# Fetching more of the gathered source rows by plain DMAs from SyncE and ScalarE in a two-layer graph kernel

## The reference

```python
h = relu(layernorm(x))
# layer 1
edge_in  = concat([h[src], h[dst], edge_attr])            # 128 + 128 + 64
edge_msg = relu(relu(edge_in @ We1 + be1) @ We2 + be2)    # 32, then 128
h2       = relu(concat([h[dst], edge_msg]) @ Wn1 + bn1)   # 64
node_msg = relu(h2 @ Wn2 + bn2)
x = x + h + segment_sum(node_msg, dst)
h = relu(layernorm(x))
# layer 2
msg = ((h @ W[etype])[src] + b[etype]) * edge_weight      # 8 relations
x = x + h + relu(segment_sum(msg, dst))
```

## Time and profile before

| what | before |
|---|---|
| median of 3 runs | 7919.92 us (7915.28 to 7920.59) |
| the profiled execution: time, span of its instructions | 7916.95 us, 7915.1 us |
| PE busy | 6812.1 us (86%) |
| POOL busy | 5850.2 us (74%) |
| DVE busy | 4295.3 us (54%) |
| ACT busy | 2361.7 us (30%) |
| indirect DMAs of layer 1 and of layer 2 | 3128 and 3055, 944 ns each |
| one-row DMAs issued by SP and by ACT (layer 2) | 6272 and 3072 |
| mean granted clock of PE | 0.94 |

### The profile page before, as it was taken

How to read it: one execution, slowest core, us unless ns; L and a number is a source line. 1 busy time by engine, 2 the same in 40 slices (tenths; PEclk the granted TensorE clock), 3 DMA queues, 4 the chain that set the end, 5 groups by cost and what they waited for, 6 DMA issues and landing times. The chain is left out here.

```text
span 7915.1 us, 215516 instructions
## 1 busy us (share of the span) xinstructions
PE 6812.1 (86%) x53038; PEld 5262.4 (66%) x53038; DVE 4295.3 (54%) x15013; ACT 2361.7 (30%) x7307; POOL 5850.2 (74%) x6213
## 2 busy tenths in 40 slices
PE   7999999999999999999978887787888887788777
PEld 6666666666666766666666666666666666666666
DVE  5445444454444544544455555555555555555555
ACT  5444444444444444444430000000000000000000
POOL 4777777777777777777757777777777777777776
PEclk8999999999999999999988889888888889988998
DMA  5333333333333333333322222222222222222222
GB/s 145 86 87 87 86 87 86 87 87 86 87 87 86 87 86 86 87 86 87 86 84 56 56 56 56 56 56 56 56 56 56 56 56 56 56 56 56 56 56 77
DMA packets 630304, 585.32 MB, mean 74 GB/s; under 512 B 306227, under 2 KB 505147, under 8 KB 629228
## 3 DMA queue, kind: packets, MB, share of 16 engines
q0 software_dynamic: 197856, 251.86, 15.3%
q1 hardware_dynamic: 422268, 325.27, 14.1%
q10 hardware_dynamic: 9600, 1.60, 0.1%
HBM read 558.88 MB, written 19.27 MB: 73 GB/s over the span
## 5 line engine op out<-in xcount | busy, mean ns | idle before, releaser
L617 POOL DMA_INDIRECT shared<-p_tab,idx x3128 | 2952.4, 944 | 1032.2 <-issue 1029.1
L617 POOL DMA_INDIRECT rows_place<-h_tab,idx x3055 | 2883.3, 944 | 945.3 <-issue 838.5
L1220 PE MATMUL bank<-shared,rows_place 128*128 128x256 f32 x6110 | 1803.2, 446 | 613.9 <-DMA rows_place<-h_tab,idx 602.6
L1220 PEld LDWEIGHTS bank<-shared,rows_place 128*128 128x128 f32 x6110 | 1273.0, 218 | 876.8 <-DMA rows_place<-h_tab,idx 659.4
L1037 DVE SCALAR_TENSOR_TENSOR shared<-bank,key,late 128x256 f32<-128x256 f32 x3128 | 1291.8, 476 | 808.4 <-PE bank L1222 667.4
L779 ACT ACTIVATE h_place<-bank 128x256 f32<-128x256 f32 x782 | 300.4, 384 | 3474.9 <-PE bank L1222 2840.5
L1131 PE MATMUL bank<-h_sb,w_tile 128*128 128x128 f32 x6256 | 908.6, 288 | 69.3 <-DVE h_sb L941 0.9
L1131 PEld LDWEIGHTS bank<-h_sb,w_tile 128*128 128x128 f32 x6256 | 759.3, 191 | 279.4 <-DVE h_sb L941 279.4
L941 DVE TENSOR_SCALAR h_sb<-bank,be_col 128x128 f32<-128x128 f32 x782 | 273.9, 350 | 1236.5 <-PE bank L1124 1236.5
L1150 PE MATMUL bank<-wn_half,h_sb 128*128 128x128 f32 x6256 | 890.8, 285 | 0.0
L1233 PE MATMUL bank<-h_place,w_rel_sb 128*128 128x64 f32 x6256 | 848.0, 293 | 0.0
(11 more groups left out here) (96 smaller groups left out, 6362.8 us busy)
## 6 DMA issues: line engine op xcount, KB each, us to landing
rows_place<-in_dst_c SPq DMA_DIRECT2D x782, 192.0 KB
h_place<-h_tab SPq DMA_DIRECT2D x6272, 0.5 KB
shared<-in_edge_cols SPq DMA_DIRECT2D x782, 128.0 KB
shared<-p_tab,idx POOLq DMA_INDIRECT x3128
h_place<-h_tab ACTq DMA_DIRECT2D x3072, 0.5 KB
rows_place<-h_tab,idx POOLq DMA_INDIRECT x3055
qr_f<-qr_tab SPq DMA_DIRECT2D x782, 36.0 KB
idx<-in_src_t SPq DMA_DIRECT2D x393, 8.0 KB
```

What stands on the lines that cost most here:

```text
L617: pool.indirect_dma_start(out=rows_of[s][:, t, :], out_offset=None, in_=table, in_offset=bass.IndirectOffsetOnAxis(ap=idx[k][:, s * TC + t ...
L1220: pe.matmul(bank[s][:, 0:RW], there, hot_rel[s % 2][:, t, :], start=(t == 0), stop=(t == TC - 1))
```

## The change

In layer 1, loops of `LONG` = 32 chunks take the place of those of 4 and 8 (`longs`, `pipelined`). In the last chunk of each of the 24 loop bodies (i = 33) POOL fetches only tiles 2 and 3. Tile 0 is fetched by SP and tile 1 by ACT, row by row, into the new tile `fed_p` (`RowFeed`). SP spreads its 128 rows over the steps 5 to 33 of the body, ACT over the steps 3 to 31, 4 or 5 rows per step. They read the numbers 8 at a time (`NUMBERS`), ACT ahead of `relu_msg1` and the rows behind it. PE sums the last chunk's source rows in four matmuls instead of one, and waits for both engines' rows. SP loads `dst_wide` and `qr_f` for the chunk two ahead (`LEAD`), and reads the windows' first nodes four at once. It loads `idx` one quad ahead instead of two, after the first gather of the running quad has landed.

In layer 2, SP's and ACT's tiles are both those of chunk 13 of each of the 49 superchunks (the last is the one that stops at chunk 13): tile 0 by SP as before, tile 1 by ACT, now 8 rows per chunk, two chunks earlier than SP. Chunk 15 is fetched by POOL in full. ACT's numbers come with SP's in one DMA of 256. POOL issues 3080 and 3030 indirect DMAs.

```diff
@@
-    ACT_ROWS = 5
-    ACT_FED_AT = SUP - 1
+    LONG = 32
+    NLONG = (NCH - 2) // LONG
+    FED_P = 2
+    LEAD = 2
+    NUMBERS = 8
...
+        def feed_step(eng, f, lead, u, lone, after, landed):
+
+            first = FED_AT - lead - SUP + 1
+            if u - first < SUP:
+                feed(eng, f, lone, u - first, landed)
+            elif after:
+                if u == first + SUP:
+                    eng.wait_ge(fed_ids_landed, 16 * after.ids_turn + 16)
+                    hold(eng)
+                feed(eng, f, after, u - first - SUP, landed)
...
+        def longs(eng, m, step):
+            for i in range(2):
+                step(Long(m, 0, i))
+            with eng.Fori(0, NLONG) as long:
+                for i in range(2, LONG + 2):
+                    step(Long(m, long, i))
+            for i in range(2 + LONG * NLONG, NCH):
+                step(Long(m, 0, i, tail=True))
...
+        class RowFeed:
+            def load_ids(self, at):
+                self.eng.dma_start(fed_p_ids[self.f][0:1, :], src_t[:, ds((at.long * LONG + LONG + 1) * TC + self.f, 1)].rearrange("p o -> o p"),
+                                   allow_slow_non_contiguous=True).then_inc(fed_p_ids_landed[self.f], 16)
+            def rows_at(self, at):
+                k = at.i - self.first if at and at.feeds else -1
+                return range(k * P // self.steps, (k + 1) * P // self.steps) if 0 <= k < self.steps else range(0)
+            def read_numbers(self, at):
+                for p in self.rows_at(at):
+                    if p % NUMBERS == 0:
+                        self.numbers[p:] = nc.values_load_multi_w_load_instructions(
+                            fed_p_ids[self.f][0:1, p:p + NUMBERS], engines=(self.eng.engine,), min_val=0, max_val=NPAD - 1,
+            def fetch(self, at):
+                for p in self.rows_at(at):
+                    self.eng.dma_start(fed_p[p:p + 1, self.f, :], p_tab[ds(self.numbers[p], 1), :]).then_inc(fed_p_landed[self.f], 16)
...
+                def load_window(at):
+                    c = chunk_of(m, at)
+                    s = c.slot
+                    sp.wait_ge(hot_built[s], c.turn + 1)
+                    hold(sp)
+                    sp.dma_start(dst_wide[s], dst_c[ds(c.i, 1), :].rearrange("c e -> (c e)").partition_broadcast(3 * W))\
+                      .then_inc(dst_wide_landed[s], 16)
+                    if s == 0:
+                        starts[:] = nc.values_load_multi_w_load_instructions(
+                            base_i[0:1, ds(c.i, SL)], engines=(sp.engine,), min_val=0, max_val=TOP,
+                    sp.wait_ge(split_hi[s], c.turn + 1)
+                    hold(sp)
+                    sp.dma_start(qr_f[s][:, :], qr_tab[ds(starts[s], W), :].rearrange("(a w) o -> a w o", a=1).broadcast_to([3, W, QR]))\
+                      .then_inc(qr_landed[s], 16)
+                feed_p = RowFeed(sp, 0, SL + 1, LONG + 1)
+                def step(at):
...
                     sp.dma_start(ea[s][:, :], edge_cols[ds(c.i, 1), :, :].rearrange("c p n -> (c p) n")).then_inc(ea_landed[s], 16)
+                    if s == 2 and at.i // SL + 1 < NQ:
+                        sp.wait_ge(prow_landed[0], 16 * TC * c.turn + 16 * TC)
+                        hold(sp)
+                        load_idx(c.quad + 1, 1 - at.i // SL % 2, idx_landed)
+                    if at.i + LEAD < NCH:
+                        load_window(Long(m, at.long, at.i + LEAD))
+                    if at.feeds and at.i == 2:
+                        feed_p.load_ids(at)
...
+                    feed_p.read_numbers(at)
+                    feed_p.fetch(at)
...
+            feed_p = RowFeed(act, 1, 3, LONG - 1)
...
+                feed_p.read_numbers(at)
                 if c:
                     relu_msg1(c)
+                feed_p.fetch(at)
                 if before:
                     relu_msg2(before)
...
+                feed_step(act, 1, 2, u, lone, after, act_row_landed)
...
+                if at.fed:
+                    for f in range(FED_P):
+                        pe.wait_ge(fed_p_landed[f], 16 * P * at.turn + 16 * P)
+                        pe.matmul(ps_h1[f * H1:(f + 1) * H1, 0:P], fed_p[:, f, :], ident[:, :], start=False, stop=True)
+                    for t in range(FED_P, TC):
+                        ins = pe.matmul(ps_h1[t * H1:(t + 1) * H1, 0:P], prow[s][:, t, :], ident[:, :], start=False, stop=True)
```

More of the change, by code:

```diff
@@ L373, in tiles_gathered @@
                 return TC * c.turn + TC
[L374 to L388, removed]
@@ L390, in pipelined @@
-        def pipelined(m_, eng, step):
[L393 to L404, removed]
+            return (c.m * (TC * SLOT_USES[c.slot] - 2 * (NSUP + 1)) + lone.k * (TC * SUP // SL - 2)
+                    + (TC * (u // SL + 1) - 2 * (u >= FED_AT)))
@@ new lines, in feed @@
+        def feed(eng, f, lone, piece, landed):
+            _, at = nc.values_load_multi_w_load_instructions(
+                fed_ids[lone.half][0:1, f * P + piece * FED_ROWS:f * P + (piece + 1) * FED_ROWS], engines=(eng.engine,),
+                min_val=0, max_val=NPAD - 1, skip_runtime_bounds_check_because="a source node's number is below the number of nodes")
+            for k, row in enumerate(at):
+                p = piece * FED_ROWS + k
+                eng.dma_start(fed_rows[p:p + 1, lone.half, f, :], h_tab[ds(row, 1), :]).then_inc(landed[lone.half], 16)
@@ L494, in step @@
                     sp.dma_start(ea[s][:, :], edge_cols[ds(c.i, 1), :, :].rearrange("c p n -> (c p) n")).then_inc(ea_landed[s], 16)
[L495 to L507, removed]
+                    if s == 2 and at.i // SL + 1 < NQ:
[6 more added lines that the diff above has]
+                        feed_p.load_ids(at)
+                    if at.feeds and at.i == SL + 1:
+                        sp.wait_ge(fed_p_ids_landed[0], 16 * at.turn + 16)
+                        hold(sp)
+                    feed_p.read_numbers(at)
+                    feed_p.fetch(at)
+                for i in range(LEAD):
+                    load_window(Long(m, 0, i))
+                longs(sp, m, step)
                 for s in range(SL):
@@ L532, in _ @@
             passes = number_of_passes(sp)
-            for k in range(HB):
-                sp.wait_ge(h_stored[k], 16 * ((NG - k + HB - 1) // HB))
             def load_ids(lone):
-                sp.dma_start(fed_ids[lone.half], src_t[:, ds((lone.k * SUP + FED_AT) * TC, 1)].rearrange("p o -> o p"),
+                sp.dma_start(fed_ids[lone.half], src_t[:, ds((lone.k * SUP + FED_AT) * TC, 2)].rearrange("p o -> o p"),
                              allow_slow_non_contiguous=True).then_inc(fed_ids_landed, 16)
[L541 to L548, removed]
             def layer1_pass(m):
-                FIRST = FED_AT - SUP + 1
                 def step(c, u, k, two, lone, after):
@@ L762, in _ @@
                     normalise_mid(g - 1)
-            def feed(piece):
-                first = piece * ACT_ROWS
-                _, at = nc.values_load_multi_w_load_instructions(
-                    act_fed_ids[0:1, first:min(first + ACT_ROWS, P)], engines=(act.engine,),
-                    min_val=0, max_val=NPAD - 1, skip_runtime_bounds_check_because="a source node's number is below the number of nodes")
-                for k, row in enumerate(at):
-                    act.dma_start(act_fed_rows[first + k:first + k + 1, :], h_tab[ds(row, 1), :]).then_inc(act_row_landed, 16)
             def copy_sums(c, u, k, two, lone, after):
```

134 lines of the change are left out of this document (75 added, 59 removed).

## The result

| what | before | after |
|---|---|---|
| median of 4 runs each, side by side | 7917.60 us | 7964.07 us (7957.19 to 7969.24) |
| ratio | 1 | 1.0058, 95% interval 1.0044 to 1.0072 |
| span of the profiled execution | 7915.1 us | 7962.8 us |
| layer 1, POOL's first to last gather | 3905 us | 3984 us |
| 32 chunks of layer 1 (one loop body of the changed kernel) | 159.8 us | 163.7 us |

The kernel became 46 us slower where 89 us of gain were forecast. Layer 2 gained 32 us as forecast. Layer 1, which should have gained 58 to 60, lost 79.

The account below looks back on a forecast made before the run. The prediction took POOL's indirect gathers to bound both layers: 91.1 us for fewer gathers, less 2 for PE ending layer 1 later, gave 89 us of gain and a median of 7831 us, range 7822 to 7908.

Parts of the forecast that it names:

- POOL's terms: Both layers: fewer gathers save 59.9 us in layer 1 and 31.2 in layer 2, together 91.1, if POOL never waits.
- PE's sum: Layer 1: PE needs 152.8 us per 32 chunks, 4.5 under POOL's 157.3.
- the 2 us taken off the sum: End of layer 1: PE finishes further behind POOL, which cuts the gain from 91.1 to 89 us.
- The loop's way back: Layer 1's 32-chunk loop: the branch back costs 2.5 us per body and doesn't reach POOL.
- ACT's rows: Layer 1: five rows delay `relu_msg2` by 0.2 to 0.3 us; cost nothing, uncovered 0.3 us per chunk at most.
- layer 2: Layer 2: 25 fewer gathers save 31.2 us; ACT holds at 4.1 to 4.7 us per chunk against POOL's 4.84.
- SP's sum in layer 1: Layer 1: SP's work per 32 chunks comes to 154.9 us against POOL's 157.3.
- Rival 3: SP bounds layer 1, making the kernel slower from 161.1 us per body; 7989 us taken, chance 0.09.
- The other bound: SP in layer 1: priced by layer 2's whole busy time, 4.51 us per block, the sum is 160.5 us.
- Rival 5: SP's number reads in layer 1 take twice their 779 ns: 167.4 us per body, 8073 us, chance 0.01.
- what a late SP costs: Layer 1: the wait ahead of `idx` costs nothing, its issue and landing under 3 us; without that cover POOL would stop.
- rivals 1 and 3: Layer 1: the first has SP or PE take back part of the gain, 7867 us, at most 7908, chance 0.19.

Follow-up runs that it names:

- e4d: Changed kernel with SP issuing 112 rows per layer 1 body instead of 128 and ACT 144: 7824.30 us, 0.9885 of before.
- g2: Changed kernel with SP issuing 112 rows, ACT 144, and `idx` fetched a step later without the wait for gathers: 7826.14 us, 0.9890 of before.
- b1: The kernel before, unchanged, run once for its trace beside the follow-up kernels: 7917.44 us.
- g1: Changed kernel with SP issuing 144 rows per layer 1 body and ACT 112: 8246.20 us, 1.0419 of before.
- f1: Changed kernel with `idx` fetched a step later, at the quad's fourth chunk, without the wait for gathers: 7934.97 us, 1.0022 of before.
- f3: Changed kernel edited so SP reads each block of 8 numbers twice; the second read isn't in its trace: 7975.80 us, 1.0071 of before.
- a1: The changed kernel itself, unedited, on chips where before takes 11,630 to 11,790 us: 1.0296 of before.

## Why the prediction was wrong

**Right: POOL's terms.** 91.1 us for 48 and 25 gathers, less 2. With SP out of the way (e4d beside before) the gain is 7914.5 - 7824.3 = 90.2 us, and the time, 7824, is within 7 us of the predicted 7831. In the trace of g2, POOL's first to last gather is 59.2 us shorter than in b1 in layer 1 and 31.7 us in layer 2, for a forecast 59.9 and 31.2.

**Right: PE, ACT and the loops in layer 1.** PE's sum, 152.8 us, stays hidden behind 157.3; where PE catches up in a body, DVE's first relu comes every 4.64 to 4.65 us, as in the earlier trace rows. PE ends layer 1 2.7 us behind POOL's last gather in e4d and 4.2 before, so the 2 us taken off the sum for it weren't needed. The loop's way back costs SP 2.6 us for a forecast 2.5, and POOL nothing. ACT's rows cost nothing in layer 1, with 144 as with 128.

**Right: layer 2.** ACT's rows don't bound; from 4200 to 7900 us SP waits 222.6 us for the gathers, and 274.0 before.

**Wrong: SP's sum in layer 1.** The step is "16 blocks of 8 rows with their reading of 8 numbers: ... 4.16 us per block, 66.6 us". The price came from layer 2, where SP's reads take 779 ns at the median. In layer 1 the same read takes a median of 1027 ns, and on ACT 723. One source line of the changed kernel, 1000 to 3000 us (min/median/max ns):

```profile
L465 ACTq TENSOR_LOAD <-fed_p_ids x197: 715/723/742, 999.7 to 2992.8; - x197
L465 SPq TENSOR_LOAD <-fed_p_ids x196: 801/1027/1097, 1004.4 to 2990.8; - x196
```

From the starts of SP's instructions over 20 bodies (417 to 3687 us), without its waits, per body:

| term | forecast | measured |
|---|---|---|
| 16 reads of 8 numbers | 12.9 | 16.7 |
| 128 rows | 53.7 (0.420 each) | 56.2 (0.439 each) |
| all else, the way back included | 88.3 | 89.5 |
| sum | 154.9 | 162.4 |

The rows of a forecast block are 4.16 less one read with its gap, 0.81. Half of the miss is the read, a third the row; the rest lies in all else and isn't divided further. The expectations above still put the sum at 161.2.

Rival 3 named the mechanism and the point: slower from 161.1 us per body. Measured are 162.4 by this table and 162.6 by the waits, some 1.4 us past it. Its price follows: 7831 + 24 x (162.6 - 157.3) = 7958 us, measured 7964. What failed was its chance, 0.09, and the choice of the sum's low end: "it holds index loads and branches that the sum already has, so I take the low end and keep 160.5 for the range". The other bound was too low as well. With 2.4 us between the sum and POOL's pace, an error of 5% in the sum decided the sign, and the duration of the read was taken from another place of the program than the one where it would stand. Rival 5 had the direction (reads dearer in layer 1), at twice instead of 1.3 times.

What that place is, the traces show, the one before included. A read's duration goes with what SP did right before it. In layer 2 of before (4200 to 7850 us), 490 reads behind a one-row DMA have a median of 782 ns, 141 behind `idx` 720 ns, 47 behind a wait 685 ns, and 46 behind the DMA that loads the numbers 970 ns. One of these 46 is the 965 ns that stands as the longest in the earlier trace rows, where the prediction took the median and noted each number as under 100 ns. Here it is with the transfer ahead of it, from SP's timeline and its source line:

```profile
6040.34 0.58 SPq L538 DMA_DIRECT2D h_place<-in_src_t  x1
...
L543 SPq TENSOR_LOAD <-h_place x1: 965/965/965, 6041.0 to 6041.0; - x1
```

In layer 1 of the changed kernel 184 of 196 reads (1000 to 3000 us) stand right behind the transfer of `qr_f`, and take 969 to 1097 ns; the 12 behind a wait take 801 to 827. In g1, where that wait is longer, 11 reads behind it take 699 to 709.

```profile
1023.99 0.81 SPq L571 DMA_DIRECT2D qr_f<-qr_tab  x1
...
L465 SPq TENSOR_LOAD <-fed_p_ids x1: 1075/1075/1075, 1024.8 to 1024.8; - x1
```

So the read isn't dearer in layer 1 as such, but behind that transfer. No run moved the reads to another place of the step, so whether that would have saved the difference isn't tested.

**Wrong in form: what a late SP costs.** "That gather lands as PE sums its chunk ... issue and landing cost under 3. I cost the wait at nothing; without that cover it would be POOL that stops." The wait did cost nothing in e4d. But with SP at its limit it is POOL that stops. From `idx`'s issue at 1072.46 to POOL's next gather at 1076.73 are 4.27 us, not under 3. POOL's periods are over their usual length by 138 us in 24 bodies, 5.7 us per body, and SP's work is over POOL's by 5.3. So the price per body was in the main SP's work, and `idx` the place where it showed; f1 gives 1.5 us of it back.

**Signs.** The prediction asked for "SP's waits in layer 1 down from 1277 to some 60 us". They fell to 25, nearer to the "near nothing" that it had named as the sign of rivals 1 and 3.

## What to carry to other kernels

When work is moved from the bound to an engine that issues transfers, sum that engine's whole stream for one loop body, with waits, register instructions and the way back, and compare the sum with the bound's. If they are closer than the prices are known, the sign isn't known either: make the split a constant and try both sides; here the sum was 5% too low. Take the price of an instruction from places where it stands behind the same kind of instruction as it will in the new loop, and look at the longest of a row as well as at its median. An engine that only issues looks idle in the shares; its room is in the view of its waits, and its lateness comes out as waits of other engines, here POOL's for the index table.

## What the runs showed of the hardware

- One instruction that reads 8 numbers into registers took SP 685 ns behind a wait, 782 ns behind a one-row DMA (both layer 2 of before), 970 ns behind the DMA that loads the numbers, and 1027 ns behind `qr_f` (layer 1, after). ACT's took 723 ns in layer 1, where its last DMA issue always ended more than 1.2 us before. Why a read is longer right behind some transfers stays open; the run meant to vary the reads (f3) didn't. SP's read of one number took 432 ns (layer 1, before), of four numbers 473 ns (layer 1, after).
- PE's mean granted clock over 200 to 3960 us fell from 1.00 to 0.97, and was 0.98 in e4d, whose body is as short as POOL's 126 gathers. In the changed kernel PE idles 2.5 us once per body. The lower clock costs nothing in e4d, where PE's 4.64 us per chunk lie under POOL's 4.99.
- Some chips run these kernels half as long again. In a1, SP's one-row DMA has the same median, 225 ns, but single register instructions of SP reach 1.4 us, where the same line's longest took 0.11 us in the trace of the result:

```profile
L471 SPq DMA_DIRECT2D fed_p<-p_tab x1110: 2/225/1195, 1000.7 to 2995.7; - x185
L471 SPq FUSED_REGOPS  x1109: 3/37/1445, 1000.7 to 2995.3; - x185
```

There the split of 112 to 144 rows gained nothing over before (1.003 to 1.006), since POOL isn't the bound. Why those chips differ isn't settled here.
